# First cross attention: scores in two 64-row halves, taken by turns over two key tiles, with three score banks

## The reference

```python
q = _ln((x @ Wq + bq).reshape(b, s1, H, HD), qn_w, qn_b)
kv = jnp.concatenate([y_main @ Wk + bk, y_main @ Wv + bv], axis=-1).reshape(b, s2, H, 2 * HD)
k = _ln(kv[..., :HD], kn_w, kn_b)
v = kv[..., HD:]
s = jnp.einsum('bhqd,bhkd->bhqk', q, k) * SCALE
p = jax.nn.softmax(s, axis=-1)
ctx = jnp.einsum('bhqk,bhkd->bhqd', p, v)
```

## Time and profile before

| | before |
|---|---|
| median of 3 runs | 2640.07 us (2638.02 to 2644.95) |
| the profiled execution, its own time | 2640.4 us, span 2638.6 us |
| PE busy | 2371.9 us (90%) |
| PE weight loads busy | 1912.3 us (72%) |
| DVE / ACT / POOL busy | 63% / 44% / 39% |
| first score to last score of stage x0b | 140.0 to 851 us |

### The profile page before, as it was taken

How to read it: one execution, slowest core, us unless ns; L and a number is a source line. 1 busy time by engine, 2 the same in 40 slices (tenths; PEclk the granted TensorE clock), 3 DMA queues, 4 the chain that set the end, 5 groups by cost and what they waited for, 6 DMA issues and landing times. The chain is left out here.

```text
span 2638.6 us, 43489 instructions
## 1 busy us (share of the span) xinstructions
PE 2371.9 (90%) x15316; PEld 1912.3 (72%) x15316; DVE 1667.7 (63%) x2670; ACT 1167.3 (44%) x2108; POOL 1039.0 (39%) x724
## 2 busy tenths in 40 slices
PE   4599999999999599996997899999999998788866
PEld 2588887878887388884776688888888876566644
DVE  3458777777878333334542388878888883666663
ACT  1334444444444233332322376766676662332242
POOL 3158777867877300000110055554455550100230
PEclk8699999999999699997998999999999998899979
DMA  3000000000000112112322000000000001211200
GB/s 108 1 26 26 26 1 26 26 13 15 26 1 1 54 60 64 64 36 52 77 49 105 24 18 26 26 18 18 19 26 26 1 1 64 62 42 38 77 0 17
DMA packets 104268, 89.74 MB, mean 34 GB/s; under 512 B 32752, under 2 KB 82432, under 8 KB 104080
## 3 DMA queue, kind: packets, MB, share of 16 engines
q1 hardware_dynamic: 103792, 87.28, 10.9%
q0 software_dynamic: 288, 0.00, 0.0%
HBM read 86.22 MB, written 1.05 MB: 33 GB/s over the span
## 5 line engine op out<-in xcount | busy, mean ns | idle before, releaser
L2179 POOL TENSOR_TENSOR xT<-xT,x1b_ring 128x512 f32<-128x512 f32 (+1 forms) x176 | 249.2, 1416 | 213.3 <-ACT x1b_ring L2309 207.0
L864 POOL TENSOR_TENSOR x0b_krstd<-x0b_krstd,minus_half 128x24 f32<-128x24 f32 x64 | 267.0, 4172 | 128.8 <-DVE x0b_krstd L928 96.5
L884 POOL TENSOR_TENSOR xT<-xT,x0b_ring 128x512 f32<-128x512 f32 (+1 forms) x176 | 248.8, 1414 | 116.9 <-ACT x0b_ring L1073 105.7
L1073 ACT ACTIVATE x0b_ring<-x0b_ring 128x512 f32<-128x512 f32 (+1 forms) x208 | 131.0, 632 | 235.4 <-DVE x0b_ring L956 227.6
L820 PE MATMUL x_ps<-x0b_qbd,x0b_kT 128*128 128x256 f32 (+1 forms) x832 | 231.9, 402 | 0.0
L111 DVE TENSOR_TENSOR x1b_plo<-x1b_ring,x1b_phi 128x512 fp32r<-128x512 f32 (+1 forms) x208 | 221.5, 1065 | 6.8 <-issue 4.6
L978 DVE TENSOR_TENSOR x0b_ring<-x_ps,x0b_krstd 128x512 f32<-128x512 f32 (+1 forms) x208 | 143.0, 687 | 93.7 <-PE x_ps L820 83.1
L2324 ACT ACTIVATE x1b_ring<-x_ps,x1b_keymask 128x512 f32<-128x512 f32 (+1 forms) x208 | 143.1, 688 | 131.2 <-DVE xT L2251 125.9
L116 PE MATMUL x_ps<-x1b_qy,x1b_yT 128*128 128x512 f32 (+1 forms) x416 | 175.9, 423 | 4.3 <-ACT x1b_ring L2324 2.9
L988 DVE TENSOR_TENSOR xT<-xT,x0b_ring 128x512 f32<-128x512 f32 (+1 forms) x176 | 165.4, 940 | 6.0
L2251 DVE SCALAR_TENSOR_TENSOR xT<-x_ps,x1b_keymask,xT 128x512 f32<-128x512 f32 (+1 forms) x176 | 131.3, 746 | 58.4 <-PE x_ps L118 57.5
(11 more groups left out here) (580 smaller groups left out, 5810.3 us busy)
## 6 DMA issues: line engine op xcount, KB each, us to landing
x_y<-in_ctx_dram SPq DMA_DIRECT2D x8, 1536.0 KB
x_y<-in_ctx_dram SPq DMA_DIRECT2D x24, 512.0 KB, 4.0
a_wn<-in_L_attn_W_Q_dram SPq DMA_DIRECT2D x16, 256.0 KB, 3.1
a_wn<-in_L_attn_W_K_dram SPq DMA_DIRECT2D x16, 256.0 KB, 3.5
a_wn<-in_L_attn_W_V_dram SPq DMA_DIRECT2D x16, 256.0 KB, 4.1
a_won<-in_L_attn_W_O_dram SPq DMA_DIRECT2D x16, 256.0 KB, 2.9
x1a_wq<-in_L_xattn_Wq_dram SPq DMA_DIRECT2D x4, 1024.0 KB, 10.6
x1c_wo<-in_L_xattn_Wo_dram SPq DMA_DIRECT2D x8, 512.0 KB, 7.0
```

Source lines behind the costliest of these rows:

```text
L864: ins = g_.tensor_tensor(r, r, c.minus_half[:, 0:8].unsqueeze(1).broadcast_to([P, whole, 8]), ALU.pow)
L884: g_.tensor_tensor(total[half][0:m, :], old, src, ALU.add).then_inc(summed, 1)
L2179: g_.tensor_tensor(total[half][0:m, :], old, src, ALU.add).then_inc(summed, 1)
```

## The change

Three things change in this stage.

The scores of a tile are made of 4 products instead of 2: group g, rows 64r to 64r+63 of kT against columns 128r to 128r+127 of qbd, which leaves out the half of the block diagonal that is zero. In step n the products on the upper half (r=1) of tile n alternate with those on the lower half (r=0) of tile n+1, which go to another bank; the score banks are now three (0, 1, 2). kT is wider, so that the last tile too has 128 columns (zeros beyond key 1585).

The row chains lose their own bank. The flips of maxima and sums and the spread of the inverse take their places in the round of three banks (now 5, 6, 7), and give them back when VectorE has read them.

The normalising moves from one step after the spread of the inverse into the same step (steps 4 and 17). The tail is one step shorter.

The diff:

```diff
...
-        kT = st.sb("kT", [P, 2, MAIN0])
+        kT = st.sb("kT", [P, 2, KT * P])
...
-        S_BANK, O_BANK, M_BANK, X_BANK, KV_BANKS = 0, 2, 4, 7, (3, 5, 6)
+        S_BANKS, O_BANK, M_BANK, KV_BANKS = (0, 1, 2), 3, 4, (5, 6, 7)
...
-        for seq in range(-1, B):
-            part = "before" if seq < 0 else "last" if seq == B - 1 else "body"
-            for ahead, e in [x for n in range(TILES) for x in ([(1, e) for e in AHEAD.get(n, [])] if seq < 0 else
-                                                               made_at(part, n))]:
-                bank = KV_BANKS[sum(uses) % len(KV_BANKS)]
-                place[seq + ahead, e] = bank, uses[bank]
-                uses[bank] += 1
+        def put(name):
+            bank = KV_BANKS[sum(uses) % len(KV_BANKS)]
+            place[name] = bank, uses[bank]
+            uses[bank] += 1
+        for e in BEFORE:
+            put((0, e))
+        for seq in range(B):
+            part = "first" if seq == 0 else "last" if seq == B - 1 else "body"
+            for n in range(TILES + 18 if part == "last" else TILES):
+                for what, at in (("sums", 29), ("inverse", 30), ("maxima", 13)):
+                    f = half_at(part, n, at)
+                    if f is not None:
+                        put((what, 2 * seq + f))
+                for ahead, e in made_at(part, n):
+                    put((seq + ahead, e))
...
-        scored, kept, max_done = st.sem("scored"), st.sem("kept"), st.sem("max_done")
+        begun, scored, kept, max_done = st.sem("begun"), st.sem("scored"), st.sem("kept"), st.sem("max_done")
...
-                for n in range(TILES + 19 if part == "last" else TILES):
+                for n in range(TILES + 18 if part == "last" else TILES):
...
+                def begin_scores(seq, n):
+                    half, kt = n // KT, n % KT
+                    if kt == 0:
+                        pe.wait_ge(q_placed, 8 * seq + (4 * half + 4))
+                    if kt in (0, 3, 6, 9):
+                        pe.wait_ge(k_done, 16 * seq + (8 * half + 2 * (kt // 3) + 2))
+                    if TILES * seq + n >= len(S_BANKS):
+                        pe.wait_ge(kept, TILES * seq + n - len(S_BANKS) + 1)
+                def scores(seq, n, g, r):
+                    half, kt, i = n // KT, n % KT, 2 * g + r
+                    rows = slice(64 * r, 64 * r + 64)
+                    return pe.matmul(ps[:, S_BANKS[(TILES * seq + n) % len(S_BANKS)], i * P:(i + 1) * P],
+                                     kT[rows, g, kt * P:(kt + 1) * P], qbd[rows, 2 * half + g, r * P:(r + 1) * P],
+                                     start=True, stop=True)
                 def step(part, seq, n):
+                    if part == "first" and n == 0:
+                        begin_scores(0, 0)
+                        for g in range(2):
+                            mm = scores(0, 0, g, 0)
+                        mm.then_inc(begun, 1)
                     f = half_at(part, n, 15)
...
                     f = half_at(part, n, 29)
...
+                        bank, nth = place["sums", 2 * seq + f]
+                        pe.wait_ge(kv_free[bank], nth + 1)
...
-                        pe.wait_ge(rowmax_done, 3 * (2 * B if part == "last" and f == 1 else 2 * seq + f + 2))
...
-                            mm = pe.transpose(ps[:, X_BANK, t * P:(t + 1) * P], total[f % 2][:, t * P:(t + 1) * P], c.ident[:, :])
+                            mm = pe.transpose(ps[:, bank, t * P:(t + 1) * P], total[f % 2][:, t * P:(t + 1) * P], c.ident[:, :])
...
+                        pe.sem_inc(kv_full[bank], 1)
                     f = half_at(part, n, 30)
...
+                        bank, nth = place["inverse", 2 * seq + f]
+                        pe.wait_ge(kv_free[bank], nth + 1)
...
-                            mm = pe.transpose(ps[:, X_BANK, t * P:(t + 1) * P],
+                            mm = pe.transpose(ps[:, bank, t * P:(t + 1) * P],
...
+                        pe.sem_inc(kv_full[bank], 1)
...
                     if n < TILES:
-                        half, kt = n // KT, n % KT
-                        m = size(kt)
-                        if kt == 0:
-                            pe.wait_ge(q_placed, 8 * seq + (4 * half + 4))
-                        if kt in (0, 3, 6, 9):
-                            pe.wait_ge(k_done, 16 * seq + (8 * half + 2 * (kt // 3) + 2))
-                        if not (part == "first" and n < 2):
-                            pe.wait_ge(kept, TILES * seq + (n - 1))
+                        after = part != "last" or n < TILES - 1
+                        if after:
+                            begin_scores(*((seq, n + 1) if n < TILES - 1 else (seq + 1, 0)))
+                        pe.wait_ge(begun, TILES * seq + n + 1)
                         for g in range(2):
-                            mm = pe.matmul(ps[0:m, S_BANK + n % 2, g * GC:(g + 1) * GC], kT[:, g, kt * P:kt * P + m],
-                                           qbd[:, 2 * half + g, :], start=True, stop=True)
-                        mm.then_inc(scored, 1)
+                            mm = scores(seq, n, g, 1)
+                            if g == 1:
+                                mm.then_inc(scored, 1)
+                            if after:
+                                mm = scores(*((seq, n + 1) if n < TILES - 1 else (seq + 1, 0)), g, 0)
+                        if after:
+                            mm.then_inc(begun, 1)
...
                     f = half_at(part, n, 13)
...
+                        bank, nth = place["maxima", 2 * seq + f]
+                        pe.wait_ge(kv_free[bank], nth + 1)
...
-                        pe.wait_ge(normed, 2 * seq + f + 1)
...
-                            mm = pe.transpose(ps[:, X_BANK, t * P:(t + 1) * P], run[f % 2][:, t * P:(t + 1) * P], c.ident[:, :])
+                            mm = pe.transpose(ps[:, bank, t * P:(t + 1) * P], run[f % 2][:, t * P:(t + 1) * P], c.ident[:, :])
...
+                        pe.sem_inc(kv_full[bank], 1)
...
             def _(v):
...
-                        v.tensor_reduce(inv, four(ps[:, X_BANK, :]), AX.X, ALU.add).then_inc(rowsum_done, 1)
+                        bank = place["sums", 2 * seq + f][0]
+                        v.tensor_reduce(inv, four(ps[:, bank, :]), AX.X, ALU.add).then_inc(rowsum_done, 1)
...
+                        v.sem_inc(kv_free[bank], 1)
...
                     if n < TILES:
...
-                                        ps[0:m, S_BANK + n % 2, :].rearrange("p (h s) -> p h s", s=S),
+                                        ps[0:m, S_BANKS[(TILES * seq + n) % len(S_BANKS)], :].rearrange("p (h s) -> p h s", s=S),
...
-                        v.tensor_reduce(top, four(ps[:, X_BANK, :]), AX.X, ALU.max).then_inc(rowmax_done, 1)
+                        bank = place["maxima", 2 * seq + f][0]
+                        v.tensor_reduce(top, four(ps[:, bank, :]), AX.X, ALU.max).then_inc(rowmax_done, 1)
...
+                        v.sem_inc(kv_free[bank], 1)
...
-                    f = half_at(part, n, 31)
+                    f = half_at(part, n, 30)
...
+                        bank = place["inverse", 2 * seq + f][0]
...
-                            part_of = ps[rows, X_BANK, :].rearrange("p (g h n) -> p g h n", g=2, h=4)[:, :, j, :]
+                            part_of = ps[rows, bank, :].rearrange("p (g h n) -> p g h n", g=2, h=4)[:, :, j, :]
...
-                        v.wait_ge(normed, 2 * seq + f + 3)
+                        v.wait_ge(normed, 2 * seq + f + 1)
+                        v.sem_inc(kv_free[bank], 1)
...
-                v.sem_inc(normed, 2)
...
```

More of the change, by code:

```diff
@@ L775, in _ @@
                 for g in range(HG0):
-                    pe.transpose(ps[:, S_BANK, g * P:(g + 1) * P], bk[:, 4 * g:4 * g + 4, :].rearrange("p h d -> p (h d)"),
+                    pe.transpose(ps[:, S_BANKS[0], g * P:(g + 1) * P], bk[:, 4 * g:4 * g + 4, :].rearrange("p h d -> p (h d)"),
                                  c.ident[:, :])
@@ L894, in _ @@
                 v.memset(headsum[:, :], 0.0).then_inc(zeroed, 1)
+                v.memset(kT[:, :, MAIN0:KT * P], 0.0).then_inc(zeroed, 1)
                 for a in yT:
                     v.memset(a[:, :, MAIN0:MAIN0 + 1].bitcast(F32), 0.0).then_inc(zeroed, 1)
-                v.wait_ge(zeroed, 4)
+                v.wait_ge(zeroed, 5)
                 for j in range(4):
                     v.memset(headsum[32 * j:32 * j + 32, j:j + 1], 1.0).then_inc(zeroed, 1)
-                v.wait_ge(zeroed, 8)
+                v.wait_ge(zeroed, 9)
                 v.tensor_scalar(headkn[:, :], headsum[:, :], kn[:, 1:2], None, ALU.mult).then_inc(ready, 1)
@@ L1051, in _ @@
                 act.wait_ge(prepared, 1)
-                act.activation(kbias[:, :], ps[:, S_BANK, :].rearrange("p (g n) -> p g n", g=HG0)[:, :, 0], ACT.Copy)
+                act.activation(kbias[:, :], ps[:, S_BANKS[0], :].rearrange("p (g n) -> p g n", g=HG0)[:, :, 0], ACT.Copy)
```

(2 more changed lines are left out.)

2 lines of the change are left out of this document (1 added, 1 removed).

## The result

The changed kernel takes 2672.1 us (median of four runs, 2663.97 to 2675.06) against 2641.6 us for the kernel before on the same chip (2638.02 to 2644.95). The ratio is 1.0111, 95% interval 1.0083 to 1.0138. It is slower by some 29 us where 18 us less were forecast. The profiled execution took 2674.16 us with a span of 2672.4 us.

The account below looks back on a forecast made before the run. TensorE, which never rests in this stage, was taken as the bound. Shorter scores give 28.4 us, Y11's wait takes back 10.2, so 18.2 us off 2640.4: 2622 us, own range 2613 to 2632, wider range 2607 to 2640.

Parts of the forecast that it names:

- The gain of an ordinary step: Scores in ordinary steps hold TensorE 0.79 us in place of 0.97, gaining 0.18 us; 16 such steps a middle sequence.
- the twin in self attention 1: Existing 64-row products by turns, 16 loads in 1.00 us, used to price the new block of eight at 0.68 us.
- step 12: Tile with 49 keys becomes 128 wide, so the change of form goes away: 0.40 us gained.
- step 4: Flips stand before the scores; the added change of arrangement costs 0.20 us against 0.18 gained: nothing.
- steps 0, 1 and 5: In a middle sequence, counted as ordinary steps, gaining 0.18 us each.
- steps 14 and 25: Step 14's gain goes into an existing wait, so nothing; step 25, a 49-key tile, gains 0.40 us.
- the last sequence: Nothing is made ahead: 15 ordinary steps at 0.18 and four steps at 0.40 us, 4.3 us gained.
- Y11's wait: In step 17 flip Y11 waits for the inverse's bank: 1.7 us in six middle sequences, 10.2 us; upper bound 2.1 each.
- The clock: Three low stretches of 1.7 us stay; bounds none (5 us less) to one in each of seven sequences (7 more).
- rival D: More drains and Y11's wait bring further 1.2 GHz stretches in steps 15 to 18: 2658 us, chance 0.08.
- The banks: The third score bank changes no wait; chains in the round make Y11 wait, and V0 at most 0.2 us.
- the tail: After the last scores it hangs on GpSimd and ScalarE and moves as a whole.

Follow-up runs that it names:

- full rows: The changed kernel with score products on 128 rows by 256 columns as before, Y11 still in step 17: 2666.1 us, ratio 1.0097.
- turns: The changed kernel, scores on 64 rows alternating between halves, with flip Y11 moved from step 17 to 18: 2659.3 us, ratio 1.0075.
- the first probe: The changed kernel plus long blocks of one product form each: 0.056 us an instruction on 64 rows in turns, 0.112 on one half.
- The second probe: The changed kernel plus nine blocks mixing score forms with 1, 2 or 4 weak 4-column products; read by granted clock alone, no kernel time given.
- the form alone: The kernel before with only the scores on 64 rows in turns, two score banks, chains in their own bank: 2659.8 us, ratio 1.0070.
- Y11 moved: The changed kernel with scores on 128 rows as before and flip Y11 in step 18: 2644.7 us, ratio 1.0022.
- moving W: Sums of squares W03, W11, W13, W02 put one step later: 2682.2 us on 64-row scores with before's banks, 2652.8 us in the kernel before.
- one half: The kernel before with 64-row scores, all four products of a step on rows 0 to 63, result partly wrong: 2803.2 us, ratio 1.0647.

## Why the prediction was wrong

- **The gain of an ordinary step.** Forecast 0.18 us, measured 0.22. The way to it (the twin in self attention 1 for the block, a bare load behind it) was right. Undisturbed steps add up to 3.2 us a middle sequence where 3.7 were forecast: 0.18 was too little by 0.04, step 12 gave 0.35 (forecast 0.40), step 4 gave 0.22 where flips were to eat it, but steps 0, 1 and 5 gave nothing, and steps 14 and 25 became 0.20 longer. That step 12 came near is partly luck: a gain too low by 0.04 and a price of the 49 columns too high by half met in it. In step 25 the forecast was 0.6 off. It had read the earlier trace rows as the price of a change of form, and thought that the trace agreed with the page on it; the load of W02 shows that the row held a wait. It waits for ScalarE's squares, and these don't come sooner.

```profile
613.84 0.52 PEld L808 LDWEIGHTS x_ps<-x0b_qbd,x0b_kT 64*128 64x128 f32 x8
615.49 1.41 PEld L773 LDWEIGHTS x_ps<-x0b_headsum,x0b_sq 128*128 128x128 f32 x12 [1.12 <-issue]
```

  With the last sequence (4.6 us) and the first (about 1) it is 25 us in place of 28.4. That term stands.
- **Y11's wait.** Forecast six times 1.7 us, 10.2 in all; measured 12.4 us, the longest 2.1, which was the upper bound. Its mechanism is the one described. Moved away, with full rows it gives 21 us (2666.1 to 2644.7), with turns 10 to 13 (ratios 1.0111 and 1.0075, medians 2672.1 and 2659.3). With full rows that is more than its own length, as low stretches go with it: 9 against 3 (33 against 28 with turns).
- **The clock. This is the step that failed**: "The clock is left as it is: three low stretches of 1.7 us." It is 33 stretches in place of 4. The stage grew by 31.9 us. With 25 us gained and 12.4 waited for Y11, 31.9 + 25 - 12.4 = 44.5 us are left for the 29 further ones, 1.5 us each, near the 1.7 of the earlier trace rows. The argument against rival D was the 1.00 us of the 16 loads in self attention 1. That row says that the form runs at full speed there, and the first probe says the same of a pure block. It says nothing of a step in which the 64-row block stands between small products and flips. The second probe has that case, and there the forms differ.
- **The rival that came.** D had the outcome: from 15 further stretches on the kernel is slower, at three a sequence 2658. There were 29, more than three a sequence. Its cause was half right. The wait of 1.7 us accounts for 5 of them (full rows, Y11 in step 17), and the form for some 23 (the form alone, 27 against 4). It had 0.08, which was too little: the earlier trace rows showed the clock falling in half of the middle sequences already, at full rows.
- **The banks.** The third score bank was to keep the form from adding a wait, and it did: TensorE never waits for the scores to be read in the changed kernel, and with two banks the form alone waits 11 us for it. That the tail would move as a whole was wrong by 2 to 3 us. The tail was 36.7 us in the change, before 33.5.

Before, plus 6 us for banks and order (Y11 moved), plus 14 to 15 for the form (2644.7 to 2659.3), plus 10 to 13 for Y11 in step 17, is 30 to 34 us; the change's own ratio gives 29, its medians 31. None of the versions that compute all scores beats the kernel before.

What stays open: which property of the products the clock goes by. Rows, entering and leaving, or both would each explain turns falling before full rows. A version that keeps the shorter steps and the clock was not found; a fuller piece of work beside each weak one was tried only by moving W.

## What to carry to other kernels

Before products are made smaller, look at the granted clock of the stage: if it falls in some repetitions already, work that is taken out of TensorE may be paid for with more time at 1.2 GHz; here a low stretch of 3.4 us cost 1.5 to 1.7 us. Half arrays in turns reached their factor of two in a long block only; entered and left each step, nearly half of the saving was lost (0.22 of 0.86 - 0.45 = 0.41 us gained). A speed seen in one stage proves the form for that surrounding only.

## What the hardware showed unexpectedly

- Blocks in which TensorE is busy for 100% of the time were granted 1.00 or 0.50 according to the form of the products between the weak ones: 45 us at 0.50 with products on one half, 26 us at 1.00 with full rows in groups of about the same length and the same weak product.
- The kernel with longer steps (one half) had twice as many low stretches as the one with shorter (64 against 27): more busy time didn't hold the clock.
- A pair of instructions of 64 rows by 128 columns, one on each half, takes 0.112 us in a long block, and a single one on one half takes the same 0.112.
